# Width-8 attentions: two heads side by side in 64-row groups of the stacked operands

## The reference

```python
# first of layer 1; then the mixture of layer 2 (four experts); then layer 3
energy = jnp.einsum('bqhe,bkhe->bqhk', q, k)
attn = jax.nn.softmax(energy, axis=-1) / sqrt(E)
out = jnp.einsum('bihv,bvhd->bihd', attn, v)
...
for e in range(e_total):            # every expert e of 4 attends over its member tokens
    att = jnp.einsum('bqhd,bkhd->bhqk', q, k) * sm_scale
    att = jnp.where(validg[:, None, None, :], att, -1000000000.0)
    att = jax.nn.softmax(att, axis=-1)
    y = jnp.einsum('bhqk,bkhd->bqhd', att, v).reshape(b, s, d)
...
q = apply_rotary(q)                 # layer 3
k = apply_rotary(k)
```

## Time and profile before

| | us |
|---|---|
| median of 3 runs | 2993.87 (2988.32 to 3002.89) |
| span of the profiled execution | 2977.2 |
| PE busy in it | 2648.4 (89%) |
| DVE busy | 1981.0 (67%) |
| ACT busy | 1625.1 (55%) |
| POOL busy | 491.0 (16%) |
| mean granted TensorE clock | 0.934 of full |

### The profile page before, as it was taken

How to read it: one execution, slowest core, us unless ns; L and a number is a source line. 1 busy time by engine, 2 the same in 40 slices (tenths; PEclk the granted TensorE clock), 3 DMA queues, 4 the chain that set the end, 5 groups by cost and what they waited for, 6 DMA issues and landing times. The chain is left out here.

```text
span 2977.2 us, 72656 instructions
## 1 busy us (share of the span) xinstructions
PE 2648.4 (89%) x21433; PEld 1793.4 (60%) x21433; DVE 1981.0 (67%) x4869; ACT 1625.1 (55%) x3951; POOL 491.0 (16%) x1072
## 2 busy tenths in 40 slices
PE   5999999977899896666999999999999976999898
...
GB/s 127 1 0 0 0 0 0 0 1 4 72 76 72 37 1 0 0 0 60 73 75 71 74 72 75 71 75 70 75 72 74 70 34 54 71 70 66 1 0 28
DMA packets 123330, 128.37 MB, mean 43 GB/s; under 512 B 17402, under 2 KB 102222, under 8 KB 123215
## 3 DMA queue, kind: packets, MB, share of 16 engines
q1 hardware_dynamic: 123214, 126.94, 15.5%
...
...
## 5 line engine op out<-in xcount | busy, mean ns | idle before, releaser
L631 DVE TENSOR_REDUCE a_rowmax<-a_psS 128x2 f32<-128x512 f32 x1536 | 995.9, 685 | 284.7 <-PE a_psS L443 261.8
L561 ACT ACTIVATE a_probs<-a_psT 128x512 f32<-128x512 f32 x1536 | 882.4, 595 | 315.8 <-PE a_psT L455 287.8
L443 PE MATMUL a_psS<-stackk,stackq 65*128 65x256 bf16 x3072 | 607.4, 280 | 85.6 <-DMA stackk<-mask_dram 39.2
L455 PE MATMUL a_psT<-stackq,stackk 98*128 98x256 bf16 x3072 | 593.5, 275 | 17.0 <-ACT a_probs L561 5.5
L443 PEld LDWEIGHTS a_psS<-stackk,stackq 65*128 65x128 bf16 x3072 | 237.1, 98 | 316.2 <-DVE a_rowmax L631 188.2
L469 PE MATMUL a_psO<-a_probs,values 128*32 128x256 f32 x6144 | 414.4, 387 | 0.0
L455 PEld LDWEIGHTS a_psT<-stackq,stackk 98*128 98x128 bf16 x3072 | 275.7, 98 | 117.3 <-ACT a_probs L561 53.4
L469 PEld LDWEIGHTS a_psO<-a_probs,values 128*32 128x32 f32 x6144 | 161.0, 109 | 148.3 <-issue 72.9
L730 POOL TENSOR_SCALAR a_negmax<-a_rowmax 128x16 bf16<-128x16 f32 x192 | 48.5, 252 | 983.6 <-DVE a_rowmax L631 983.6
L900 ACT ACTIVATE a_probs<-a_psS,a_negmax 128x256 f32<-128x256 f32 x256 | 120.4, 470 | 158.8 <-DVE a_negmax L925 158.8
L949 DVE TENSOR_SCALAR a_kT<-a_psQ,l_bqk 64x256 f32<-64x256 f32 x256 | 123.7, 483 | 78.8 <-ACT a_qT L893 76.9
...
## 6 DMA issues: line engine op xcount, KB each, us to landing
...
stackq<-a_negmaxT SPq DMA_DIRECT2D x384, 4.0 KB
```

The lines of the kernel that those rows point to most:

```text
L443: mm = pe.matmul(psS[h % 2][:, t * SEQ:(t + 1) * SEQ], stackq[0:MASK_ROW + 1, b, h, t * P:(t + 1) * P], stackk[0:MASK_ROW + 1, b, h, :], s ...
L455: mm = pe.matmul(psT[h % 2][:, t * SEQ:(t + 1) * SEQ], stackk[0:MAX_ROW + 2, b, h, t * P:(t + 1) * P], stackq[0:MAX_ROW + 2, b, h, :], sta ...
L561: act.activation(probs[:, h // 4 % 2, h % 4, :], psT[h % 2][:, :], ACT.Exp, scale=w.exp_scale).then_inc(exp_done, 1)
L631: dve.tensor_reduce(rowmax[:, s.parity(1), h, :], psS[h % 2][:, :].rearrange("p (t k) -> p t k", t=2), AX_X, ALU.max).then_inc(max_done, 1)
```

## The change

The two stacks keep their size but are laid out anew. A head has its 48 part rows, a mask row (48) and two max rows (49, 50) in a group of 64 rows: heads 0 to 7 of an operand in rows 0 to 50, heads 8 to 15 in rows 64 to 114. Four jobs' stacks fit instead of two. The slots `u` = 0 to 15 of a step run through four heads of the lower group, four of the upper, and so on.

On PE a slot now issues scores of one head as a matmul on one 64-row tile of the array and shifted scores of another job's head on the other 64-row tile, in turn (`score_pair`), and waits for the maximum, the exponential and the landed DMAs ahead of both. `scores` of slot 0 waits for all of the read-back, where it waited for half. The outputs of two heads (9 columns each, of a 32-column tile) are summed in one PSUM tile, so that `oT` and its turn (`turn_output`) come once per step, with four transposes, and DVE's `normalise` once, on twice the columns. The q and k projections move from after head 15 to slot 9. ACT only copies them with the bias to float32 `raw` (slot 9). POOL does all of the split, one step ahead (offset 3), the high part included, and with rotary the two products and their sum as well (DVE's before). Tokens are copied one step earlier. SP's step is now: save of job `s+2`, max rows of slots 8 to 15, the whole read-back (12 DMAs, 14 with the mask), max rows of slots 0 to 7. The save waits also for the read-back before it to have landed. The weights' columns, and so the rows of `scratch`, are ordered (group, d, head) where they were (d, head); the 8 heads of a row are still 4 KB, and rows follow each other without a gap. The fill of the constant rows at the start takes six DMAs for three. The diff, cut:

```diff
 HEADS = 16
 HD = 8
 SLOT = 32
-BF_ROWS = 48
-MASK_ROW = 64
-MAX_ROW = 96
+PAIRS = HEADS // 2
+GROUP_ROWS = 64
+MASK_ROW = 48
+MAX_ROW = 49
+ZERO_ROW = 51
+LEAD = 4
 EXPERTS = 4
...
 
-    jobs, unroll, first = BATCHES * weights, max(2, weights), 4
-    plan = Plan(jobs, weights, unroll, first, rounds=(jobs - 3 - first) // unroll, drain=1)
-
-    plan.misc_uses = [("o2", -1), ("m1", 0), ("o3", -1), ("v", 1), ("y", -1), ("o0", 0), ("m0", 1), ("out", -1), ("o1", 0)]
-
-    plan.misc_uses += [("qk", 3)] + ([("qk2", 3)] if rotary else [])
+    jobs, unroll, first = BATCHES * weights, 4, 4
...
+            def save(s):
+                wait_alone(sp, parts_ready, s.n(2, 1, 1), sp_passed)
                 if s.known(2, 1):
-                    wait_alone(sp, scores_ready, s.n(1, HEADS, 8 * half + 1), sp_passed)
-                src = scratch[b].rearrange("qk part (d h) t -> qk part d h t", h=HEADS)
-                for repeats, part, row in ((3, 0, 0), (2, 1, 24), (1, 2, 40)):
-                    rows = slice(row, row + 8 * repeats)
-                    sp.dma_start(stackq[rows, b, hs, :], src[0, part, :, hs, :].unsqueeze(0).to_broadcast([repeats, HD, 8, SEQ])).then_inc(stack_ready[half], 16)
-                    sp.dma_start(stackk[rows, b, hs, :], src[1, 0:repeats, :, hs, :]).then_inc(stack_ready[half], 16)
-                if masked:
-                    row = m.mask_dram[s.batch(2), s.expert(2)]
-                    sp.dma_start(stackk[MASK_ROW:MASK_ROW + 1, b, hs, :],
-                                 row.unsqueeze(0).unsqueeze(0).to_broadcast([1, 8, SEQ])).then_inc(stack_ready[half], 16)
-
-            def step(s):
+                    wait_alone(sp, stack_ready, s.n(2, stack_inc), sp_passed)
+                sp.dma_start(scratch[s.parity(2)].rearrange("qk part p t -> p qk part t"),
+                             parts[:, :, :, :]).then_inc(parts_saved, 16)
+
+            def stack(s):
+
+                b = s.quarter(2)
+                wait_alone(sp, parts_saved, s.n(2, 16, 16), sp_passed)
+                if s.known(2, 4):
+                    wait_alone(sp, shifted_ready, s.n(-2, HEADS, HEADS), sp_passed)
+                src = scratch[s.parity(2)].rearrange("qk part (g d h) t -> qk part g d h t", g=2, h=PAIRS)
+                for g in range(2):
+                    for repeats, part, row in ((3, 0, 0), (2, 1, 24), (1, 2, 40)):
+                        rows = slice(GROUP_ROWS * g + row, GROUP_ROWS * g + row + 8 * repeats)
+                        sp.dma_start(stackq[rows, b, :, :], src[0, part, g, :, :, :].unsqueeze(0).to_broadcast([repeats, HD, PAIRS, SEQ])).then_inc(stack_ready, 16)
+                        sp.dma_start(stackk[rows, b, :, :], src[1, 0:repeats, g, :, :, :]).then_inc(stack_ready, 16)
+                    if masked:
+                        row = m.mask_dram[s.batch(2), s.expert(2)]
+                        r = GROUP_ROWS * g + MASK_ROW
+                        sp.dma_start(stackk[r:r + 1, b, :, :],
+                                     row.unsqueeze(0).unsqueeze(0).to_broadcast([1, PAIRS, SEQ])).then_inc(stack_ready, 16)
+
+            def step(s):
+                if s.has(2):
+                    save(s)
                 if s.has(0):
                     max_rows(s, 0, 1)
                 if s.has(2):
-                    wait_alone(sp, parts_ready, s.n(2, 1, 1), sp_passed)
-                    if s.known(2, 2):
-                        wait_alone(sp, stack_ready[1], s.n(2, stack_inc, -stack_inc), sp_passed)
-                    sp.dma_start(scratch[s.parity(2)].rearrange("qk part p t -> p qk part t"),
-                                 parts[:, :, :, :]).then_inc(parts_saved, 16)
-                    wait_alone(sp, parts_saved, s.n(2, 16, 16), sp_passed)
-                    if s.known(2, 2):
-                        wait_alone(sp, shifted_ready, s.n(0, HEADS, 8), sp_passed)
-                    stack(s, 0)
+                    stack(s)
                 if s.has(1):
                     max_rows(s, 1, 0)
-                if s.has(2):
-                    if s.known(2, 2):
-                        wait_alone(sp, shifted_ready, s.n(0, HEADS, 16), sp_passed)
-                    stack(s, 1)
 
             pipeline(sp, plan, step)
...
+            def scores_part(s, u, t):
+                half, i, j = group_of(u)
+                r, pr, b = GROUP_ROWS * i, 4 * half + j, s.quarter(1)
+                return pe.matmul(psS[u % 2][:, t * SEQ:(t + 1) * SEQ], stackq[r:r + MAX_ROW, b, pr, t * P:(t + 1) * P],
+                                 stackk[r:r + MAX_ROW, b, pr, :], start=True, stop=True, tile_position=(r, 0))
+
+            def shifted_part(s, u, t):
+                half, i, j = group_of(u)
+                r, pr, b = GROUP_ROWS * (1 - i), 4 * half + j, s.quarter(0)
+                return pe.matmul(psT[u % 2][:, t * SEQ:(t + 1) * SEQ], stackk[r:r + ZERO_ROW, b, pr, t * P:(t + 1) * P],
+                                 stackq[r:r + ZERO_ROW, b, pr, :], start=True, stop=True, tile_position=(r, 0))
+
+            def score_pair(s, u):
+
+                if s.has(1):
+                    if u == 0:
+                        pe.wait_ge(stack_ready, s.n(1, stack_inc, stack_inc))
+                    if s.known(1, 1) or u >= 2:
+                        pe.wait_ge(max_done, s.n(1, HEADS, u - 1))
+                if s.has(0):
+                    if u % 8 == 0:
+                        pe.wait_ge(maxrow_ready[u // 8], s.n(0, 32, 32))
+                    if s.known(0, 1) or u >= 2:
+                        pe.wait_ge(exp_done, s.n(0, HEADS, u - 1))
                 for t in range(2):
-                    mm = pe.matmul(psS[h % 2][:, t * SEQ:(t + 1) * SEQ], stackq[0:MASK_ROW + 1, b, h, t * P:(t + 1) * P],
-                                   stackk[0:MASK_ROW + 1, b, h, :], start=True, stop=True)
-                mm.then_inc(scores_ready, 1)
-
...
 
             def step(s):
-                for h in range(HEADS):
-                    if s.has(1):
-                        scores(s, h)
-                    if s.has(0):
-                        shifted(s, h)
-                    if h == 1 and s.has(-1):
-                        turn_output(s, -1, 2)
-                    if h == 2 and s.has(-1):
+                for u in range(HEADS):
+                    score_pair(s, u)
+                    if u == 2 and s.has(-1):
                         prob_values(s, -1, 3)
-                    if h == 4 and s.has(0):
+                    if u == 4 and s.has(0):
                         turn_max(s, 0, 1)
-                    if h == 5 and s.has(-1):
-                        turn_output(s, -1, 3)
-                    if h in (6, 10, 14) and s.has(0):
-                        prob_values(s, 0, (h - 6) // 4)
-                    if h == 7 and s.has(1):
+                    if u == 5 and s.has(-1):
+                        turn_output(s)
+                    if u in (6, 10, 14) and s.has(0):
...
+                    if u == 8 and s.has(-1):
                         turn_y(s)
-                    if h == 9 and s.has(0):
-                        turn_output(s, 0, 0)
-                    if h == 10 and s.has(1):
-                        turn_max(s, 1, 0)
-                    if h == 12 and s.has(-1):
-                        project_out(s)
-                    if h == 13 and s.has(0):
-                        turn_output(s, 0, 1)
-                    if h == 15 and s.has(3):
+                    if u == 9 and s.has(3):
                         project_qk(s, "qk", w.wq, w.wk)
                         if rotary:
                             project_qk(s, "qk2", w.wq2, w.wk2)
...
-                    if h in (7, 11, 15) and s.has(0):
-                        copy_oT(s, 0, (h - 7) // 4)
+                        exponential(s, u)
+                    if u == 2 and s.has(-1):
+                        copy_oT(s, -1, 1)
+                    if u == 9 and s.has(3):
+                        copy_qk(s, "qk", 0)
+                        if rotary:
+                            copy_qk(s, "qk2", 1)
+                    if u == 11 and s.has(0):
+                        copy_oT(s, 0, 0)
...
+                    wait_alone(pool, parts_saved, s.n(3, 16), pool_passed)
+                pool.tensor_copy(parts[:, :, 0, :], whole).then_inc(high_ready, 1)
+                wait_alone(pool, high_ready, s.n(3, 1, 1), pool_passed)
+                pool.tensor_tensor(rest[:, :, :], whole, parts[:, :, 0, :], ALU.subtract).then_inc(rest_ready, 1)
+                wait_alone(pool, rest_ready, s.n(3, 1, 1), pool_passed)
                 pool.tensor_copy(parts[:, :, 1, :], rest[:, :, :]).then_inc(middle_ready, 1)
-                wait_alone(pool, middle_ready, s.n(2, 1, 1), pool_passed)
+                wait_alone(pool, middle_ready, s.n(3, 1, 1), pool_passed)
                 pool.tensor_tensor(parts[:, :, 2, :], rest[:, :, :], parts[:, :, 1, :], ALU.subtract).then_inc(parts_ready, 1)
...
+            def step(s):
+                if s.has(0):
```

(8 more changed lines are left out.)

330 lines of the change are left out of this document (157 added, 173 removed).

## The result

The changed kernel takes **3536.28 us**, the median of four runs (3534.19 to 3540.28), beside 2991.89 for the kernel before (four runs): a ratio of 1.1805, 95% interval 1.1782 to 1.1828. It is 18% slower. Its four executions differ by 6 us.

The account below looks back on a forecast made before the run. SP's chain and the transfers were taken as a bound as tight as PE. Per step 4.3 + 1.75 + 0 + 14.1 gave a period of 20.15 us, +350 in all; with +56 for the clock, 2993.9 became 3400 us, range 3100 to 3600.

Parts of the forecast that it names:

- the likeliest case: Whole kernel: the forecast itself, a longer circle through SP and the transfers, 3300 to 3500 us, chance 0.52.
- term (4): First read-back issue to the next step's first matmul: 14.1 us, ends 12.5 to 16.2, before 7.37.
- (1): SP's circle, step start to issue of the max rows: 4.3 us, before 4.70.
- term 5: Granted clock: half the steps begin at half clock, 1.2 us each, +56 us in all, ends 0 and +112.
- (2): SP's circle, max rows to the first read-back: same two DMAs and two waits, 1.75 us.
- (3): The save, now at the step's start: 0 us on the circle, before 3.11; POOL ends long before the next step.
- A: Read-back: the DMAs' form doesn't decide the engines, transfers stay spread, 3150 us, chance 0.13.
- B: Whole step: faster, read-back lands within 9.4 us and PE decides, period 15.5 us, 2915 us, chance 0.03.
- C: Read-back: worse still, each 4 KB run takes 0.20 us, 2.5 us more per step, 3576 us, chance 0.20.
- D: PE slots: scores and shifted scores run one after another, tiles don't overlap, +56 us, 3456 us, chance 0.09.

Follow-up runs that it names:

- awake: Changed kernel plus six unused fp32 matmuls behind slot 15 of every step, to fill PE's idle stretch before slot 0: 3481.36 us.
- second combination: Changed kernel with `stackk` and `stackq` rows spread, work through read-back a step earlier, each read-back group behind a pair of max rows: 2895.43 us, timed ratio 0.9652.
- order: Changed kernel with group 0 read back ahead of the max rows of slots 8 to 15, group 1 behind them: 3545.32 us.
- first combination: Changed kernel with `stackk` rows spread, work through read-back a step earlier, group 1 read back before the first max rows, group 0 after: 3230.16 us.
- form run: Kernel before with two unused rows behind each scratch part, giving wide `stackk` DMAs the changed kernel's form: 3243.08 us against 2999.64.
- spread run: Changed kernel with scratch keeping a group's parts together, so wide `stackk` DMAs read plain rows 4 KB apart; save becomes two DMAs: 3184.51 us.

## Why the prediction was right, and where its terms were off

The direction, the mechanism (wide reads on few engines lengthen SP's circle) and the range (3100 to 3600) hold. The 3400 was 136 us too low, and the result lies above the likeliest case's own range, 3300 to 3500: the cost of the clock was put at a third of what it is, and the DMAs that end the step were left out of term (4).

**What bounds.** "SP's chain and the transfers are a bound as tight as PE" holds. A change that took work off every engine but POOL made the circle longer, and the kernel with it.

**(1) Step start to max rows, 4.3.** Measured 5.77. At full clock it is 4.07, in the steps of awake that have it, and 4.20 in the second combination. The rest is term 5.

**(2) Max rows to read-back, 1.75.** Measured 1.65.

**(3) The save, 0.** Right: issued 0.4 us before the step starts and landed by 2300.7, 3.5 us before the max rows. Its new wait ends where I put it in `a2`, with the landing of the read-back (2320.90, save at 2320.99). In `a3` it waits for POOL's last part and is issued 0.6 us into the step, still long before the max rows. That POOL ends long before the next step is not so there, and in the runs order and first combination it cost what I had put at nothing.

**(4) Read-back to the next step, 14.1.** Measured 15.29, inside 12.5 to 16.2. The reading of the tail, two engines at 25 GB/s for what the wide forms put on few engines, is what the form run and the spread run bear out. Two things were missed. From the first issue to the last landing there are 14.94 us, and with 1.5 before the first traffic some 13.4 for the transfers in place of 11.7. And what ends the wait are the max rows behind them, 0.35 later: I had left their issue and landing out of term (4), although they are issued last in every step. That read-back alone is not the end became plain only when a step of slack changed nothing.

By the rule of the Trainium skill ("DMA: Bandwidth & Descriptors", section "Why a DMA increments its semaphore by 16 and not by 1") the counts of engines, 3 and 2 in place of 12 and 16, fit the increments, 82 against 126. The sum by it, 0.5 us a step less than mine, would have missed by more: it gives the runs on the busiest engine, not what lies between them.

**(5) The clock, +56.** This term was wrong twice. "I count half the steps" should have been all of them: all 58 steps looked at in `a2` begin at half clock. And 1.2 us for such a step was too little: the steps of awake give 1.70 (5.77 against 4.07), so that 93 steps cost some 158 us, above my upper end of 112.

Per step of `a2` the period is 2.6 us above the 20.15: -0.23 in term (1) at full clock, +1.70 by the clock, -0.10 in (2) and +1.19 in (4). I had added 0.6 of it as clock. With the smaller misses of `a1` and `a3`, 1.98 x 63 + 1.35 x 15 + 0.96 x 15 make 160 us too little. That it came to 136 is in part luck: the stages' starts cost 10 us and not 20, and the median lies 3.6 us above the changed kernel's span, where I had 16.7 for the kernel before.

**The rivals.** A, transfers stay spread: excluded by the form run, and it names what it would have been worth (3184.51 with them spread, 3150 forecast). B: the runs reached its period only with all rows spread and another order of the work, 15.32 against the 15.5 I had worked out for `a2`. Its sum has a slip: 15.5 in `a3` would give (17.15 - 15.5) x 15 = 25 where it has 8; `a3` stayed at 17.09. C, worse still (3576): the nearest in time, with half of its 2.5 us in term (4); whether a 4 KB run takes 0.20 us or the engines stand still between runs isn't separated. D: excluded by the rows, scores and shifted scores start together (2302.29 both, and within 0.03 us in all pairs of `a2`).

**What costs nothing.** Right, and too timid in one place: that the chain of `stackq` could be spread as well was in the rows of before, where its wide issues cost 0.74 and 0.67, and was worth 145 us in the changed layout. Right, too, is that the copies and turns taken off lie beside the chain, as far as the shares of ACT and DVE show; no run tested them one by one.
